# One-hot comparisons of chunks 1 to 3 read the row number from SBUF instead of PSUM

## The reference

```python
e = stack([tbl_f[ids[:, f]] for f in range(26)], axis=1)         # 2048 x 26 x 128
sd = einsum('bfd,bd->bf', e, dense)                              # dense row with each embedding
ss = einsum('bfd,bgd->bfg', e, e)                                # embeddings with each other
z = concatenate([dense, sd, ss[:, iu, ju]], axis=1)              # upper triangle, 325 pairs
h = concatenate([z, dense], axis=1)
h = relu(h @ W_top1 + b_top1)
h = relu(h @ W_top2 + b_top2)
y = h @ W_top3
```

## Time and profile before

| | before |
|---|---|
| median of 3 runs | 391.6 us (390.85 to 392.52) |
| the profiled execution's own time | 391.02 us |
| its span on the core | 389.2 us |
| TensorE busy | 348.4 us (90%) |
| GpSimd busy | 264.3 us (68%) |
| VectorE busy | 242.9 us (62%) |
| ScalarE busy | 190.6 us (49%) |
| mean granted TensorE clock | 0.952 |

### The profile page before, as it was taken

The page is one execution under the profiler, slowest core; times in us unless marked ns, Lnnn a source line. Parts: engine busy times, 40 slices in busy tenths (PEclk is TensorE's granted clock), DMA queues, the critical chain, the costliest instruction groups (busy, mean ns, idle before and its releaser), DMA issues.

```text
span 389.2 us, 12471 instructions
## 1 busy us (share of the span) xinstructions
PE 348.4 (90%) x5471; PEld 269.9 (69%) x5471; DVE 242.9 (62%) x475; ACT 190.6 (49%) x299; POOL 264.3 (68%) x279
## 2 busy tenths in 40 slices
PE   2899985999999999999999989999999988346996
PEld 0566664877788877777788878776788876235773
DVE  0789996877888644887987446886986341101420
ACT  3356664768323337577143157674133169822333
POOL 6777775777777777777777777777777777771000
PEclk9999998999999998999999998999999989756899
DMA  7999212333333232343223222433431222220000
GB/s 189 247 233 216 49 47 93 89 86 88 112 85 81 83 74 62 90 99 105 85 84 105 78 61 52 117 90 90 110 80 54 54 56 58 57 53 20 3 0 0
DMA packets 20107, 33.41 MB, mean 86 GB/s; under 512 B 7916, under 2 KB 10488, under 8 KB 20055
## 3 DMA queue, kind: packets, MB, share of 16 engines
q0 software_dynamic: 8704, 17.84, 18.2%
q1 hardware_dynamic: 11351, 14.78, 14.3%
HBM read 32.60 MB, written 0.01 MB: 84 GB/s over the span
## 4 chain that ended last, share of the span: by engine, by line
PE 37%; POOL 8%; issue 4%; ACT 3%; DMA 1%; DVE 1%; POOLq 0%; ACTq 0%; DVEq 0%
PE late_bank L599 9%; POOL rows L498 8%; PE gram_bank L561 5%; PE turn_bank L542 3%; PE turn_bank L522 3%; PE turn_bank L523 3%; PE late_bank L522 2%; PE late_bank L523 2%; PE spare_bank L635 2%; ACT turned L349 2%; DMA rows<-in_tbl_dram,index 1%; PE gram_bank L635 1%; PE turn_bank L579 1%; PE late_bank L647 1%; PE gram_bank L579 1%
## 5 line engine op out<-in xcount | busy, mean ns | idle before, releaser
L498 POOL DMA_INDIRECT rows<-in_tbl_dram,index x272 | 263.5, 969 | 87.1 <-issue 79.5
L915 DVE TENSOR_TENSOR one_hot<-table_ids,row_number 125x512 fp32r<-125x512 int32 x216 | 134.4, 682 | 27.3 <-PE turn_bank L523 15.4
L349 ACT COPY turned<-turn_bank 128x512 f32<-128x512 f32 (+1 forms) x72 | 70.9, 1029 | 47.1 <-PE turn_bank L542 47.0
L542 PE MATMUL turn_bank<-ident,rows 128*128 128x128 f32 x288 | 48.2, 302 | 21.2 <-DMA rows<-in_tbl_dram,index 11.2
L522 PE MATMUL late_bank<-one_hot,table_hi 125*128 125x512 f32 x144 | 61.8, 429 | 0.9 <-DVE table_lo L996 0.9
L561 PEld LDWEIGHTS gram_bank<-turned 128*27 128x27 f32 x4096 | 46.9, 110 | 22.4 <-issue 19.9
L561 PE MATMUL gram_bank<-turned 128*27 128x26 f32 x4096 | 56.2, 197 | 5.8 <-issue 5.3
L542 PEld LDWEIGHTS turn_bank<-ident,rows 128*128 128x128 f32 x288 | 36.9, 155 | 31.4 <-issue 16.6
L523 PE MATMUL late_bank<-one_hot,table_lo 125*128 125x512 f32 x144 | 58.3, 405 | 0.0
L319 DVE COPY gram<-gram_bank 124x208 f32<-124x208 f32 x32 | 12.0, 374 | 59.3 <-PE gram_bank L561 59.0
L522 PE MATMUL turn_bank<-one_hot,table_hi 125*128 125x512 f32 x96 | 38.8, 404 | 1.0 <-DVE one_hot L913 1.0
(11 more groups left out here) (84 smaller groups left out, 400.9 us busy)
## 6 DMA issues: line engine op xcount, KB each, us to landing
table_ids<-in_ids_by_table_dram SPq DMA_DIRECT2D x27, 256.0 KB, 3.3
rows<-in_tbl_dram,index POOLq DMA_INDIRECT x272
turned<-in_tbl_dram SPq DMA_DIRECT2D x6, 448.0 KB, 13.7
looked_up<-in_tbl_dram SPq DMA_DIRECT2D x3, 448.0 KB, 6.5
rows<-in_r_dense_features_dram SPq DMA_DIRECT2D x16, 64.0 KB
gram<-in_W_top_dram SPq DMA_DIRECT2D x1, 702.0 KB
gram<-in_W_top_dram SPq DMA_DIRECT2D x1, 512.0 KB
turned<-in_tbl_dram SPq DMA_DIRECT2D x6, 52.0 KB
```

Of the source, the lines that this page charges most:

```text
L349: copy(to[:, f0:f1], of).then_inc(rows_copied[n % 2], 1)
L498: pool.indirect_dma_start(out=rows[:, row % RING_ROWS, :], out_offset=None, in_=tables[f], in_offset=bass.IndirectOffsetOnAxis(ap=index[:, ...
L542: last = pe.transpose(turn_bank[n % 2][:, f - f0, :], rows[:, (tile * ROWS + f) % RING_ROWS, :], ident[:])
L915: last = nc.vector.tensor_tensor(hot, table_ids[0:RK, (chunk.n * LOOKUPS + s) % ID_SLOTS, 0:wide], row_number[0:RK, k:k + 1].broadcast_to( ...
```

## The change

The comparisons of all four chunks become the `tensor_scalar` form. Those of chunks 1 to 3 take the int32 ids of `table_ids` and, as the second operand, `row_number_sb[:, k]` from SBUF. The PSUM tile `row_number` and the cast that fills it are dropped, and the wait for the two casts becomes a wait for one. Which comparison is made when, and what it waits for, stay as they are.

```diff
-        row_number = ctx.enter_context(nc.psum_tensor("row_number", [P, BANK], F32))
...
                     hot = one_hot[:, n % HOT_SLOTS, 0:wide]
-                    if chunk.n == 0:
-                        last = nc.vector.tensor_scalar(hot, id_slot(s), row_number_sb[:, k:k + 1], None, ALU.is_equal)
-                    else:
-                        last = nc.vector.tensor_tensor(hot, table_ids[0:RK, (chunk.n * LOOKUPS + s) % ID_SLOTS, 0:wide],
-                                                       row_number[0:RK, k:k + 1].broadcast_to([RK, wide]), ALU.is_equal)
+                    ids_of = id_slot(s) if chunk.n == 0 else table_ids[0:RK, (chunk.n * LOOKUPS + s) % ID_SLOTS, 0:wide]
+                    last = nc.vector.tensor_scalar(hot, ids_of, row_number_sb[:, k:k + 1], None, ALU.is_equal)
                     last.then_inc(one_hot_made, 1)
...
             dve.wait_ge(numbers_made, 1)
-            nc.vector.tensor_copy(row_number[0:RK, 0:K_ROWS], row_number_int[:]).then_inc(numbers_ready, 1)
             nc.vector.tensor_copy(row_number_sb[:], row_number_int[:]).then_inc(numbers_ready, 1)
-            dve.wait_ge(numbers_ready, 2)
+            dve.wait_ge(numbers_ready, 1)
```

## The result

The changed kernel takes 401.17 us (median of four runs, 398.46 to 402.62) against 391.77 us of the kernel before (390.85 to 392.52): a ratio of 1.023, with a 95% interval from 1.018 to 1.028. It is 9.4 us slower.

What follows compares the result with a forecast made beforehand. GpSimd's unbroken gathers, ending 38 us before the end, were taken to bound the kernel. Profiled 391.0 plus 9.1 for lengthened gathers plus 0 gave 400.1, or 400.7 us with the median's 0.6; range 396 to 411.

Steps and rivals of the forecast that it cites:

- The bound: Whole kernel: from 61 us GpSimd's gathers run without a stop, and the last one plus some 38 us sets the end.
- VectorE's saving: Comparisons of chunks 1 to 3: 682 to 476 ns each, 44 us less VectorE time, worth 0 to 0.5 us at the end.
- GpSimd's loss: Gathers beside the 216 comparisons of chunks 1 to 3: lengthened by 0.042 us per comparison, 9.1 us in all.
- the sum of 400.7 us: Whole kernel: profiled 391.0 plus 9.1 plus 0 gives 400.1; the runs' median being 0.6 higher, 400.7 us.
- the thin part of chunk 0: Gathers from 10 to 30 us, beside 27 comparisons: 0.032 us lost per comparison, the lower rate behind the chosen middle.
- The upper end: Gathers from 69 to 306 us: 82 hit, each held for half a comparison, 0.238 us; 19.5 us in all.
- The tail: Stretch after the last gather: still 38 us, with that gather at 360 us instead of 351.
- rival 1: Tail or full stretches of chunks 1 and 2: TensorE's lower clock adds to the loss, about 6 us, 407; chance 0.10.
- The mechanism as I told it: Gathers meeting one-tensor SBUF VectorE instructions are held until these finish; two-operand comparisons with PSUM do not slow them.
- the prediction's 3.0 us: Lengthened gathers from 61 us on in the kernel before, put down to VectorE's copies of looked-up rows, one per chunk.
- rival 2: Gathers beside comparisons: every comparison hits like the copy of looked-up rows, 52 us, 443 in all; chance 0.02.
- the copy's rate: VectorE's copy of looked-up rows: 1.35 us long, it cost a gather 0.69 us, half its length.

Runs made afterwards that it cites:

- e12: Kernel before, old comparisons, with 48 GpSimd memsets of 128x128, one after every fourth gather of tiles 3 to 14: 395.64 us, ratio 1.008.
- e3: Kernel before with the new comparison form in chunk 1 only, the old form kept in chunks 2 and 3: 395.32 us, ratio 1.007.
- e9: Kernel before with two of each tile's 17 gathers replaced by plain DMAs of the tables' first 128 rows: 380.13 us, ratio 0.968.
- e10: Changed kernel with two of each tile's 17 gathers replaced by plain DMAs of the tables' first 128 rows: 379.05 us, ratio 0.966 to the kernel before.
- e2: Kernel before, comparisons of chunks 1 to 3 still two-tensor, but with the row number broadcast from SBUF instead of PSUM: 408.2 us, ratio 1.039.
- e1: Kernel before with chunks 1 to 3 in the new tensor_scalar form, but the row number still read from PSUM: 400.47 us, ratio 1.020.
- e4: Kernel before with chunk 0's comparisons also in the old two-tensor form, float ids from SBUF, row number from PSUM: 401.5 us, one run.
- e5: Kernel before with two of each tile's 17 gathers replaced by plain DMAs, on the slow chip: 654.76 us, ratio 0.975.

## Why the prediction was right

**The bound.** "The end is the last gather plus a tail of some 38 us" held, with tails of 38.2 to 40.9 us in the traces taken where the kernel before takes 391 to 393 us. In e12 a delay of GpSimd alone moved the last gather by 3.2 us and the median time by 3.1; in e3 a delay that ended at 137 us was still whole at the end; with 32 gathers less (e9, e10) the change cost nothing.

**VectorE's saving.** I put a comparison at 476 ns; the median was 486 and the mean 510 (GpSimd also holds VectorE, as told under e2: the longest took 728 ns and began 0.67 us after a gather; chunk 0 has such a one too). The saving was 31 us and not 44. In e9 and e10, where the cost is gone, nothing clear of noise is left of it, as predicted.

**GpSimd's loss.** The deciding term was 216 x 0.042 = 9.1 us. Measured in the profile: 10.6 us beside the comparisons, 0.049 each, and the last gather 9.8 us later, since the gathers beside the copies happened to lose 0.7 us less. That the sum of 400.7 us came within 0.5 us of the median is in part luck. The same form cost 0.041 us per comparison in e1 and 0.055 in e3, so the middle between the thin part of chunk 0 and the whole of it was right in size, but the choice within 0.032 to 0.064 had only the spacing of the groups behind it. The upper end, in which each gather that starts during a comparison is held for half of it, was twice too high. In the trace 70 gathers began during one, not 82. The 29 that began 0.1 to 0.2 us after its start grew by 0.18 to 0.32 us each, to 6.6 us in sum; the 19 that began sooner grew by 0.08 us on average, the 22 that began later by 0.02.

**The tail.** Predicted unchanged; in the profiled execution it grew by 1.8 us at a granted clock of 0.82 in place of 0.90. This looks like rival 1 in a small size, but it isn't shown that the change did it: e2's trace has a tail of 40.5 us and e12's one of 40.9 with the old comparisons and a last gather only 3.2 us later, while e1's, with a last gather 8.2 us later, has 38.8. The median execution was 1.5 us shorter than the profiled one, and since only the profiled one has a trace, how much of the 9.4 us is clock in the median can't be told.

**The mechanism as I told it.** "Beside the one-tensor form and not at all beside the two-operand form with PSUM" was right; the step from there to the fast form as the only one that disturbs, which I took into e2, was wrong. "The gather is held until the VectorE instruction is done" is too coarse as well. One of the four gathers behind the prediction's 3.0 us started at 227.25 us, before its copy (227.56 to 228.94), took 1.57 us and ended 0.12 us before it. By e2 it is VectorE's reads from SBUF that disturb in the two-tensor form. What GpSimd does at the two places where it is held, reading the row indices or writing something, no run labels: that is argued and not shown. A slip without weight: against rival 2 the prediction says that chunk 0 shows a tenth of the copy's rate, but its own 0.052 us is a fifth of 0.24.

## What to carry to other kernels

When GpSimd issues gathers back to back, look at whether their pace sets the end before making a VectorE instruction quicker: a form that takes 25% less VectorE time lost 2.3% here, because VectorE had slack and GpSimd had none. An operand in PSUM can be an advantage: of the four forms of the comparison, only the one with one tensor from SBUF and one from PSUM let the gathers pass. The same fast form is right where VectorE is short of time and GpSimd waits anyway, as in chunk 0 (e4, one run: 10 us).

## What was unexpected about the hardware

A VectorE instruction with two tensors from SBUF lengthens gathers beside it at least as much as the fast one-tensor form: 0.072 us for each instruction of 693 ns against 0.049 for each of 510. The two don't do it alike: the first holds a gather only as it starts, the fast form also about half-way through, and there it can be held itself. The place of the per-partition scalar makes no difference (ratio 1.020 from PSUM, 1.023 from SBUF). And one chip ran the same kernel in 668 us in place of 392; in e5's trace from there TensorE's weight loads stand idle on "issue".
